# A four-layer graph network: softmax steps counted by a drain, table steps moved, leak by group, four sum tables

## The reference, cut to what matters

```python
# 1. five graph transformer convolutions, 4 heads of 32, GELU and residual between them
alpha = sum(q[dst] * k[src]) / sqrt(32);  attn = softmax of alpha over the edges of one dst
out   = segment_sum(v[src] * attn, dst) + x @ Ws + bs
# 2. relational attention: 4 edge types, each with its own W and attention vector
alpha = leaky(a_dst[type, dst] + a_src[type, src], 0.2); softmax over (type, dst)
out   = segment_sum(x_rel[type, src] * w, dst)
# 3. two GCN layers with symmetric degree norm, ELU between
# 4. weighted scatter: z = x @ W
out   = leaky(segment_sum(z[src'] * edge_weight, dst') + bias, 0.01)
```

## Time and profile before

| | us |
|---|---|
| median of 3 runs | 6402.66 |
| lowest and highest | 6401.93, 6410.21 |
| the profiled execution, device time | 6401.28 |
| its span in the trace | 6399.0 |
| TensorE busy | 3841.5 (60%) |
| VectorE busy | 3430.5 (54%) |
| ScalarE busy | 1622.5 (25%) |
| GpSimd busy | 3902.0 (61%) |
| mean granted TensorE clock | 0.657 of 2.4 GHz |

### The profile page before, as it was taken

One profiled execution on the slowest core, in us unless ns is written; L12 is line 12 of the kernel. 1 busy time (PEld: TensorE's weight loads), 2 busy tenths in 40 slices (PEclk: granted clock), 3 DMA queues, 4 the chain that ended last, 5 costly groups with the idle time before them and its releaser, 6 DMA issues. The chain is left out here.

```text
span 6399.0 us, 89877 instructions
## 1 busy us (share of the span) xinstructions
PE 3841.5 (60%) x18940; PEld 3122.8 (49%) x18941; DVE 3430.5 (54%) x9637; ACT 1622.5 (25%) x3734; POOL 3902.0 (61%) x3751
## 2 busy tenths in 40 slices
PE   3576656665767566658886566664443444555554
PEld 2466445544665465536663465653333333444443
DVE  5566556654665466646654777744334434544441
ACT  3243324332333143325453222220000000211110
POOL 0777267735774577547751655607775776488882
PEclk9677767776777677768886555555555555655557
DMA  7666266626662656356644333201111111566654
GB/s 235 198 177 181 62 204 181 179 69 195 178 178 86 178 175 179 105 163 181 176 117 109 73 68 69 61 16 52 52 52 46 52 52 43 111 106 105 107 88 112
DMA packets 793860, 763.52 MB, mean 119 GB/s; under 512 B 173985, under 2 KB 668722, under 8 KB 793138
## 3 DMA queue, kind: packets, MB, share of 16 engines
q0 software_dynamic: 199680, 383.63, 24.5%
q1 hardware_dynamic: 548338, 353.77, 19.1%
q10 hardware_dynamic: 45504, 22.55, 1.3%
HBM read 660.61 MB, written 98.87 MB: 119 GB/s over the span
## 5 line engine op out<-in xcount | busy, mean ns | idle before, releaser
L599 POOL DMA_INDIRECT kvconv<-kv_tab,src_all x1664 | 1629.5, 979 | 1035.3 <-POOLq L632 529.2
L599 POOL DMA_INDIRECT rowsg_<-h_tab,src_all x832 | 793.6, 954 | 457.6 <-issue 252.9
L1807 POOL DMA_INDIRECT sum_tab<-ysw_,idxw_ x416 | 650.3, 1563 | 140.5 <-issue 120.7
L599 POOL DMA_INDIRECT rows_r<-rel_tab,idx_r x416 | 417.5, 1004 | 422.5 <-POOLq L1097 161.0
L599 POOL DMA_INDIRECT kvlast<-kv_tab,src_all x416 | 410.3, 986 | 241.3 <-issue 122.5
L817 ACT ACTIVATE Sconv<-s8conv 128x512 f32<-128x512 fp8e4 x416 | 261.0, 627 | 387.6 <-PE pA1conv L779 273.2
L877 DVE TENSOR_TENSOR msgconv<-kvconv,sm_attEconv 128x512 f32<-128x512 f32 x416 | 285.9, 687 | 123.1 <-PE pA0conv L779 58.0
L779 PEld LDWEIGHTS pA0conv<-Sconv,msgconv 128*128 128x128 f32 x1664 | 302.9, 256 | 13.8
L779 PE MATMUL pA0conv<-Sconv,msgconv 128*128 128x128 f32 x1664 | 301.5, 342 | 0.0
L779 PEld LDWEIGHTS pA1conv<-Sconv,msgconv 128*128 128x128 f32 x1664 | 291.3, 247 | 17.1
L893 DVE TENSOR_REDUCE sm_alphaconv<-prodbconv 128x16 f32<-128x512 f32 x416 | 283.0, 680 | 2.4 <-DVE sm_exconv L455 0.6
(11 more groups left out here) (668 smaller groups left out, 9547.9 us busy)
## 6 DMA issues: line engine op xcount, KB each, us to landing
qwinconv<-q_tab SPq DMA_DIRECT2D x1664, 64.0 KB
st8conv<-st_tab SPq DMA_DIRECT2D x52, 512.0 KB
kvconv<-kv_tab,src_all POOLq DMA_INDIRECT x1664
s8conv<-s_tab SPq DMA_DIRECT2D x52, 512.0 KB
qwinlast<-q_tab SPq DMA_DIRECT2D x416, 64.0 KB
hwinw_<-h_tab SPq DMA_DIRECT2D x416, 64.0 KB
srcbw_<-in_src_row SPq DMA_DIRECT2D x104, 256.0 KB
sum_tab<-zero ACTq DMA_DIRECT2D x56, 256.0 KB, 3.7
```

The costliest lines, as they stand in the source:

```text
L599: nc.gpsimd.indirect_dma_start(rows[:, par * TG + t, :], None, tab, bass.IndirectOffsetOnAxis(ap=idx[:, g * TG + t:g * TG + t + 1], axis=0 ...
L1807: nc.gpsimd.indirect_dma_start(sum_tab[q % 2 * 4 + j], bass.IndirectOffsetOnAxis(ap=idx[:, t:t + 1], axis=0), ys[:, t, :], None, compute_o ...
```

## The change

Five edits.

1. **Drain.** In the six softmax steps the semaphore is no longer incremented by the last matmul but by a drain instruction behind it (`done_by`), in all convolutions and in the relational layer.
2. **Table steps.** The setup block keeps only xT, the source indices, the bases and the identities (`constants`). The rest moves with the one-hot tables into `tables`, which runs between the projection and the edges of convolution 0; that layer is now written out ahead of a loop over layers 1 to 3. The one-hot matrix is built in 104 instructions of one quad instead of 13 of one group, and the reset vectors are made after it with fewer links between instructions. During `tables` GpSimd gathers groups 0 and 1 of convolution 0.
3. **Zero fill.** It moves to the edges of the first GCN layer.
4. **Leak.** In the relational layer the parts are laid out so that the reduce reads runs of twelve; it writes `alpha` directly, and the source's score and the leak are applied once a group, in quad 7, instead of in each quad.
5. **Sum tables.** Four instead of eight. Tile j of every quad goes to table j, each scatter waits for the one before it on its table, and GpSimd's loop is written out.

```diff
+SUMS = 4
+    def done_by(pe, name):
+        nc.tensor.drain().then_inc(sem(name), 1)
...
-                                ident[:, :]).then_inc(sem(tag + "lt"), 1)
+                                ident[:, :])
+            done_by(pe, tag + "lt")
...
+        def constants():
...
+                        sp.dma_start(xT[:, :], xT_in).then_inc(there, 16)
+                        sp.dma_start(src_all[:, :], src_c).then_inc(there, 16)
+                        sp.dma_start(base_i[:, :], first_row).then_inc(there, 16)
+                        sp.wait_ge(there, 48)
...
+        def tables(kv):
...
+                    @block.gpsimd
+                    def _(pool):
+                        for g in range(2):
+                            gather_group(pool, "c_", 0, g, g, kv_tab, src_all, kv)
...
+                            for q in range(QG):
+                                t = g * TG + 4 * q
+                                v.tensor_tensor(s8[:, g % 2, 4 * q:4 * q + 4, :], iota_row[:, :].unsqueeze(1).to_broadcast([P, 4, P]),
+                                                rel[:, t:t + 4].unsqueeze(2).to_broadcast([P, 4, P]),
+                                                ALU.is_equal, saturate=False).then_inc(built, 1)
...
-                    def score(g, q, par):
...
-                    def leak(g, q, par):
...
+                    def pick(g, q, par):
+                        dve.wait_ge(sem(tag + "prod"), quad(g, q) + 1)
+                        v.tensor_reduce(sm["alpha"][:, par, :, 4 * q:4 * q + 4].rearrange("p h t -> p t h"),
+                                        picked[:, :, :, :], AX.X, ALU.add).then_inc(sem(tag + "al"), 1)
+                    def leak(g, par):
+                        for q in range(QG):
+                            rows_there(dve, CONVS, halved(g, par), par, q)
+                        dve.wait_ge(sem(tag + "al"), quad(g, QG))
+                        al = sm["alpha"][:, par, :, :]
+                        v.tensor_tensor(al, al, rows[:, par * TG:(par + 1) * TG, D:D + H].rearrange("p t h -> p h t"), ALU.add
+                                        ).then_inc(sem(tag + "whole"), 1)
+                        dve.wait_ge(sem(tag + "whole"), g + 1)
+                        v.scalar_tensor_tensor(out=al, in0=al, scalar=0.2, in1=al, op0=ALU.mult,
+                                               op1=ALU.max).then_inc(sem(tag + "alpha"), QG)
...
+                    for n in range(GROUPS * QG):
+                        pool.wait_ge(sem(tag + "y_out"), n + 1)
+                        pool.wait_ge(sem(tag + "idx"), n + 1)
+                        for j in range(4):
+                            k, t = j % SUMS, 4 * (n % QG) + j
+                            if 4 * n + j >= SUMS:
+                                pool.wait_ge(sem(f"{tag}added{k}"), 16 * ((4 * n + j) // SUMS))
+                            nc.gpsimd.indirect_dma_start(
+                                sum_tab[k], bass.IndirectOffsetOnAxis(ap=idx[:, t:t + 1], axis=0),
+                                ys[:, t, :], None, compute_op=ALU.add).then_inc(sem(f"{tag}added{k}"), 16)
...
-        one_hot_tables()
-        with nc.Fori(0, CONVS - 1) as l:
-            conv_layer(l, "conv")
+        constants()
+        conv_layer(0, "conv", "conv0", first=True)
+        with nc.Fori(1, CONVS - 1) as l:
+            conv_layer(l, "conv", "conv")
```

More of the change, by code:

```diff
@@ L122, in gnn_kernel @@
         rowrB = gsb("rowrB", [R, GROUPS * H * (TG + 1)], bf16)
[L125 to L213, removed]
-                        for h in range(H):
[L215 to L218, removed]
@@ new lines, in _ @@
+                        link(v.tensor_copy(seg_f[:, :, :], seg_i[:, :, :]))
+                        for o, k in ((blocks(rstF[:, :], P), 1), (blocks(rstB[:, :], P)[:, :, ::-1], 2)):
+                            last = v.tensor_tensor(o, blocks(seg_f[:, 0, :], P), blocks(seg_f[:, k, :], P), ALU.not_equal)
+                        link(last)
+                        for o in (rstF, rstB):
+                            v.tensor_scalar(o[:, :], o[:, :], NEG, None, ALU.mult)
+                        ends = [(o, a, b, h) for o, a, b in ((blocks(rowrF[:, :], ROW), 2, 3),
+                                                             (blocks(rowrB[:, :], ROW)[:, :, ::-1], 0, 1)) for h in range(H)]
@@ new lines, in _ @@
+                        at = lambda a, h: slice(h * (TG + 1) + (a == 2), h * (TG + 1) + (a == 2) + TG)
+                        for o, a, b, h in ends:
+                            last = v.tensor_tensor(o[:, :, at(a, h)], blocks(edge_f[:, a, :], TG),
+                                                   blocks(edge_f[:, b, :], TG), ALU.not_equal)
+                        link(last)
+                        for o, a, b, h in ends:
+                            v.tensor_scalar(o[:, :, at(a, h)], o[:, :, at(a, h)], NEG, None, ALU.mult)
@@ L615, in rows_there, with gather_all @@
             eng.wait_ge(sem(f"rows{par}_{q}"), 64 * (turn * ((GROUPS + 1) // 2 - par) + half + 1))
-        def gather_all(pool, group):
-            for g in range(GROUPS):
+        def gather_all(pool, group, since=0):
+            for g in range(since, GROUPS):
                 group(g, g % 2)
@@ L1178, in _ @@
                             dve.wait_ge(stored[b % 2], 80 * (b // 2))
-                        whole = stage[:, b % 2, :, :, D + H:RW]
-                        part = [ad[:, b % 2, :, k, :].rearrange("p j (r h) -> p j r h", h=H) for k in range(3)]
-                        left = rest[:, :, :].rearrange("p j (r h) -> p j r h", h=H)
+                        whole = stage[:, b % 2, :, :, D + H:RW].rearrange("p j r h -> p j h r")
+                        part = [ad[:, b % 2, :, :, k * R:(k + 1) * R] for k in range(3)]
+                        left = rest[:, :, :].rearrange("p j (h r) -> p j h r", h=H)
                         if b >= 1:
@@ L1596, in _ @@
                     gather_all(pool, lambda g, par: gather_group(pool, tag, 0, g, par, h_tab, src_all, rows, "agg"))
+                if tag == "g1_":
+                    @block.scalar
+                    def _(act):
+                        for tab in sum_tab:
+                            for b in range(NB):
+                                act.dma_start(tab[b * BW:(b + 1) * BW, :].rearrange("(j p) f -> p j f", p=P),
+                                              zero[:, :].unsqueeze(1).to_broadcast([P, 4, D])).then_inc(sem("zeroed"), 16)
+                            act.dma_start(tab[NPAD:NPAD + P, :], zero[:, :]).then_inc(sem("zeroed"), 16)
                 @block.tensor
```

193 lines of the change are left out of this document (110 added, 83 removed).

## The result

The changed kernel takes 6343.0 us in the median of four runs (6340.8 to 6350.3), the kernel before 6404.4 in the same comparison: ratio 0.9905, with an interval of 0.9888 to 0.9922. The time is 61 us less where 82 were forecast, 22 above the 6321 that were named and inside the forecast's own range. The profiled execution has a span of 6339.0, 60.0 less than before.

The account below looks back on a forecast made before the run. GpSimd's gathers and scatters pace the edges and scatter layer; in the relational layer VectorE and TensorE alternate. Terms -33 - 32 + 4.5 + 11.7 - 2 + 2 + 1 - 34 = -82 us gave 6321 us, range 6285 to 6360.

Parts of the forecast that it names:

- parts 1, 2 and 5: Part 1, Part 5, and between them the first layer's gathers, two groups fetched early, their end moving from 533 to 501: -32 us.
- part 3: Drains in the softmax steps, 0.15 us a step on the joint chain: +4.5 us in convolutions, +11.7 in the relational layer.
- part 4: Leak by group in the relational layer: VectorE's relief mostly ends in waits, 0.15 us a group counted, -2 us.
- three signs of being wrong: Table writes and gathers hold up the builder; a drain holds TensorE over 0.3 us; GpSimd's idle time in the scatter loop grows.
- dear drain: Rival: a drain costs 0.63 us, so the drains cost 68 us instead of 16, 6373 us in all; chance 0.09.
- Part 1: Setup and one-hot tables: the first layer's edges start at 136 us instead of 168.7, -33 us.
- Part 5: Four sum tables: +2 us for late scatters, +1 for zero fill beside the GCN gathers, -34 in the summing.
- The rival of the clock: Pauses keep TensorE's clock down throughout; the last convolution grows by 147 us, 6468 in all; chance 0.03.

Follow-up runs that it names:

- a_count: The changed kernel without drains, the last matmul of each of the six softmax steps counting again: 6302.8 us, ratio 0.9844 to the kernel before.
- a_hoist: The changed kernel, drains kept, each quad's four register loads for its sums moved ahead of the preceding softmax step: ratio 0.9976, where the kernel before takes 7719 us.

## Why the prediction was right, and where it was off

The time lies in the range and the direction was right, and so were the mechanisms of parts 1, 2 and 5. The mechanism of part 3 was not, that of part 4 in part, and the loop was missing. That the sum was off by only 21 us is in part luck: the drains alone were 27.7 us dearer than said, the first layer and the summing missed by 11.5 more, and 18.2 came back from the leak, the loop and the scatters. Two of the prediction's three signs of being wrong came: the builder was held up (9.4 us in one stop), and a drain holds TensorE for more than 0.3 us. The terms, as predicted and as the traces of before, after and a_count have them:

| | predicted | measured |
|---|---|---|
| edges of the first layer begin | -33 | -28.5 |
| first layer's gathers | -32 | -28.3 |
| drains, convolutions | +4.5 | +13.4 |
| drains, relational layer | +11.7 | +30.5 |
| leak by group | -2 | -10.5 |
| scatter and zero fill | +3 | 0 |
| summing | -34 | -30.7 |
| the loop's entry | none | -6.7 |

**Part 3 is the step that failed**, "I take 0.15 us a step on the joint chain". The drain's own wait for the last matmul was rightly seen to be nearly free for the reader. The mistake was in what it does to TensorE's queue. The row that I went by shows the overlap of two matmuls, 0.06 us. It doesn't show what the queue had meanwhile done for the next block. A drain stops the queue there, and what comes after it costs 0.4 to 0.5 us ahead of scores, 0.9 to 1.0 ahead of sums. Of the latter 0.5 are register loads, as a_hoist shows; how the other 0.4 to 0.5 split between semaphore waits and the restart isn't shown. Of these 0.7 us a step on average, 0.39 are on the path in the relational layer (30.5 / 78) and 0.45 in the stretches after the last gathers (13.4 / 30). The rival *dear drain* named the upper bound of 0.63 on the path; the truth lies in the middle between it and the forecast. The prediction had said that a hold of TensorE by more than 0.3 us would make it wrong, and that a group would grow by under 1 us: against the kernel before, where it is 54.7 in the middle of the layer, it grew by 2.2.

The section "Step-by-step: what each phase is for" of the Trainium skill's page "TensorE: Matmul & The Clock Gate" says that the sequencer doesn't wait for a matmul to leave the array but takes up the next instruction. The trace agrees: 0.25 us from the turned scores to the next matmul, 0.78 when a drain forbids it. The isolated price of 175 ns, from the section "Single matmul latency", gave 19 us as an estimate; the runs show 40.

**Part 4** missed for the opposite reason. Most of VectorE's relief did vanish in its waits, as said, but less of it than counted: a group's period fell by 0.55 us on average (6.6 in twelve periods) where I had counted 0.15, and the first group's turned scores, which have no softmax beside them, came 3.5 earlier. In which quads the relief counts no run shows.

**Part 1** was 4.5 us short: the spacing was 0.631 us for 0.62, and the waits on table buffers 9.4 for 5, with 1 us gained at the projection. The sum's smaller rest came as told: reset work 18.8 us for 18, group 2 at 53.7 us for 51, the first matmul at 12.9 for 14.

**Part 5**: the six blocks lasted 5.4 us on average for 4.9; the first data came after 8.7. A scatter's four-step distance hid its landing: GpSimd waits 18.9 us for landings in all 416 scatters, and its idle time before them is 140.1 us for 140.5.

**The loop.** No step of the sum held it: with the first layer ahead of the loop, one turning point is gone, 6.7 us.

The rival of the clock did not come: the mean granted clock is 0.661 for 0.657, and the last convolution grew by 10.8 us, where it would have been 147.

## What to carry to other kernels

Count a group of matmuls by its last matmul. A drain cost the reader 0.02 us here and the engine 0.4 to 1.0, what its queue would have done ahead, so price it by what stands behind it, and if it has to be, put register loads in front. Cutting the number of tables pays where the tables are read, and was free here, where a landing of 3.6 us stands against a distance of 7.6 in the loop. Work moved beside a stream of gathers has to be priced with the gathers on, and may behave differently in another setting. A sum that comes out right may hold misses that cancel: check each term.

## What the runs showed of the hardware that was not expected

- A drain behind a drain takes 13 ns; the first takes 922 in the median, which contains the matmuls in front of it. All 468 together cost 40 us of 6343.
- A hardware loop over layers costs 4 to 6 us at each turning point in the fast setting (77.9 and 79.9 us for 73.6 and 73.8 from node stage to next gather) and 4.3 in the slow one (78.1 for 73.8). In the slow one the layers' edges are 27 us longer each in the loop as well.
- The same matmuls of the summing came at a mean granted clock of 0.81 in one kernel and 0.95 in another that doesn't differ there, and the stage took 50.1 and 45.0 us.
- The slow setting runs this kernel a fifth slower with equal durations of instructions. Its stops fall where gathers run beside the other engines' work and are absent in the scatter layer; the builder stood still for 57.9 us beside gathers and never without them. That the other engines' instructions arrive late beside the gathers' transfers would fit, but was not tested, and stays open.
